# Six graph layers on one Trainium2 core: f32 queries and keys in the first attention, centring on GpSimd, and a new order of all parts

## What is computed

```python
h = jnp.maximum(_layernorm(x, axis=-1), 0.0)
x = x + _L0_gnn_ref(h, adj, ...)   # attention, 12 heads of 32, masked by adj, beta * adj added
h = jnp.maximum(_layernorm(x, axis=-1), 0.0)
x = x + _L1_gnn_ref(h, adj, ...)   # 2 layers: exp(h W h^T) * adj, one W above and one below the diagonal
h = jnp.maximum(_layernorm(x, axis=-1), 0.0)
x = x + _L2_gnn_ref(h, adj, ...)   # 2 layers: softmax(h h^T) * adj, three value matrices (upper, diagonal, lower)
h = jnp.maximum(_layernorm(x, axis=-1), 0.0)
x = x + _L3_gnn_ref(h, adj, ...)   # attention, 12 heads, adj as bias, output projection
```

```python
q = _split_heads(input_graph @ Wq + bq)
k = _split_heads(input_graph @ Wk + bk)
scores = jnp.einsum('bhqd,bhkd->bhqk', q, k) / jnp.sqrt(jnp.asarray(HD, input_graph.dtype))
scores = jnp.where(adj_e > 0, scores + beta * adj_e, -9e15)
probs = jax.nn.softmax(scores, axis=-1)
```

## Time and profile before

| | |
|---|---|
| median of 3 runs | 2869.08 us |
| the profiled execution | 2870.44 us, of which span of the instructions 2868.4 us |
| granted TensorE clock, mean over the span | 0.991 |
| PE busy | 2745.3 us, 96% |
| DVE busy | 2475.5 us, 86% |
| ACT busy | 1797.9 us, 63% |
| POOL busy | 1396.4 us, 49% |
| DMA | 125.40 MB, 44 GB/s |

### The profile page before, as it was taken

The page is one execution under the profiler, slowest core; times in us unless marked ns, Lnnn a source line. Parts: engine busy times, 40 slices in busy tenths (PEclk is TensorE's granted clock), DMA queues, the critical chain, the costliest instruction groups (busy, mean ns, idle before and its releaser), DMA issues.

```text
span 2868.4 us, 86681 instructions
## 1 busy us (share of the span) xinstructions
PE 2745.3 (96%) x33152; PEld 2100.0 (73%) x33152; DVE 2475.5 (86%) x6886; ACT 1797.9 (63%) x6516; POOL 1396.4 (49%) x2313
## 2 busy tenths in 40 slices
PE   3799999999999999999999999999999999999996
PEld 2577777777777777777777777777777777777763
DVE  6788888888888888888888888888888888888875
ACT  6566666666666666666666666666666666666653
POOL 0345554554544554554554554554455454554553
PEclk8999999999999999999999999999999999999998
DMA  6221121221212121121221222121121221121110
GB/s 199 57 38 40 39 42 40 38 42 41 37 43 42 36 45 39 36 45 39 36 45 39 36 45 40 39 42 40 39 42 40 39 42 39 36 45 40 36 32 20
DMA packets 343428, 125.40 MB, mean 44 GB/s; under 512 B 310896, under 2 KB 342896, under 8 KB 342896
## 3 DMA queue, kind: packets, MB, share of 16 engines
q1 hardware_dynamic: 333808, 107.28, 18.9%
q10 hardware_dynamic: 9216, 12.59, 1.2%
HBM read 31.72 MB, written 12.58 MB: 15 GB/s over the span
## 4 chain that ended last, share of the span: by engine, by line
PE 85%; DVE 6%; ACT 3%; issue 2%; POOL 2%; DMA 2%; SPq 0%; POOLq 0%; ACTq 0%; DVEq 0%
PE bank L925 63%; PE bank L1030 8%; PE bank L975 5%; PE bank L991 3%; PE bank L967 3%; DMA ht<-qk 1%; PE bank L1021 1%; ACT t L672 1%; DVE t L804 1%; PE bank L980 1%; PE bank L997 1%; DVE qk L782 1%; DMA row<-in_rows_dram 1%; DVE qk L750 1%; ACT qk L648 0%
## 5 line engine op out<-in xcount | busy, mean ns | idle before, releaser
L925 PE MATMUL bank<-w_hi,ht 128*128 128x384 f16 x3840 | 1028.6, 326 | 0.2 <-ACT v L639 0.2
L925 PE MATMUL bank<-ht,w_hi 128*128 128x128 f16 x9216 | 838.4, 220 | 17.1 <-DMA ht<-qk 15.3
L925 PE MATMUL bank<-ht,w_lo 128*128 128x128 f16 x4608 | 806.5, 220 | 0.0
L925 PEld LDWEIGHTS bank<-ht,w_hi 128*128 128x128 f16 x9216 | 725.9, 98 | 79.1 <-issue 33.8
L925 PE MATMUL bank<-w_lo,ht 128*128 128x384 f16 x1920 | 626.5, 326 | 0.0
L672 ACT ACTIVATE t<-t,few 128x128 f32<-128x128 f32 x1536 | 592.4, 389 | 6.8 <-DVE few L813 4.9
L925 PEld LDWEIGHTS bank<-w_hi,ht 128*128 128x128 f16 x3840 | 375.8, 98 | 232.8 <-issue 2.0
L925 PEld LDWEIGHTS bank<-ht,w_lo 128*128 128x128 f16 x4608 | 453.5, 98 | 0.0
L551 POOL TENSOR_TENSOR h<-h,row 128x384 f32<-128x384 f32 x256 | 258.0, 1008 | 242.8 <-DVE h L904 242.8
L663 ACT ACTIVATE qk<-bank 128x256 f16<-128x256 f32 x576 | 215.6, 381 | 234.9 <-PE bank L925 234.3
L541 POOL TENSOR_TENSOR v<-v,row 128x384 f32<-128x384 f32 x256 | 259.4, 1014 | 180.9 <-ACT v L639 180.9
(11 more groups left out here) (112 smaller groups left out, 5059.7 us busy)
## 6 DMA issues: line engine op xcount, KB each, us to landing
x<-in_x_dram SPq DMA_DIRECT2D x64, 192.0 KB, 2.3
out_dram<-h ACTq DMA_DIRECT2D x64, 192.0 KB, 2.2
ht<-qk SPq DMA_TRANSPOSE x384, 2.8
w_hi<-in_weights_dram SPq DMA_DIRECT2D x9, 576.0 KB, 5.1
w_lo<-in_weights_dram SPq DMA_DIRECT2D x8, 576.0 KB, 4.9
adj<-in_adj_dram SPq DMA_DIRECT2D x64, 64.0 KB, 2.2
row<-in_rows_dram SPq DMA_DIRECT2D x1, 3456.0 KB, 15.4
spare<-in_weights_dram SPq DMA_DIRECT2D x2, 576.0 KB, 5.0
```

Source lines behind the costliest of these rows:

```text
L925: m = nc.tensor.matmul(out, a, b, start=(first and n == 0), stop=(last and n == 3 * len(left) - 1))
```

## The change

1. **Queries and keys of the first attention stay f32.** ScalarE writes them with the bias as f32 into the same tile (`QF`, the f32 view of `QK`); VectorE has no part in these `proj` steps; the bank is released by ScalarE's signal; `scores` waits for that and makes one f32 matmul for each head, 12 in place of 36. Order strings of VectorE have three entries fewer for each graph.
2. **Centring by GpSimd.** The 24 + 8 additions of the negative mean go from ScalarE to a new `set_up` of GpSimd: first w5, then the eight rows, then w8 to w14.
3. **Two row DMAs.** The eight rows that are centred come in one DMA behind w2, with a semaphore of their own, the other ten in one behind w5.
4. **New order strings** for all engines, opening, body (11 times) and closing. In the opening, SyncE issues x and `adj` of streams 2, 1 and 0 right after the biases and ahead of all weights, and the first graph's turn ahead of w4; GpSimd's set-up pieces stand ahead of the first graph's value bias; the turns of graphs 1 and 2 and their loads on the other engines come earlier. In the body, TensorE's order now has `scale` and `mix` of the last attention side by side, `aturn`, the third `vals` and `context` of DIG_B one after the other, and `flip` ahead of `scores` of the last attention; GpSimd does the masks of DIG_B's `aturn` before the norm's addition of DIR_B.

```diff
+WHOLE_QK = (GAT,)
...
 OPENING = {
...
     "sync":
-        "wwwww0ww1wwww0wwwww4w120www032w101032102143",
+        "w210wwwww0wwwwwwww1w4w3w02www0w1w0103210241",
 }
...
-REPEATS = 10
+REPEATS = 11
...
     if name == "proj":
-        return ["high", "low"]
+        return ["high"] if layer in WHOLE_QK else ["high", "low"]
...
+        if name == "proj":
+            return layer not in WHOLE_QK
...
+    if name == "proj" and layer in WHOLE_QK:
+        return "high", step, 0
     return RELEASE[name], step, j if name == "scores" else 0
...
+        QF = [q.bitcast(F32).rearrange("p (c a t) -> p c a t", c=C, a=2) for q in flat_qk]
...
                     if w == 2:
-                        sp.dma_start(row[:, 1:N_ROWS], rows_v[:, 1:N_ROWS].broadcast_to((P, N_ROWS - 1, D))).then_inc(rows_in, 16)
+                        sp.dma_start(row[:, CENTRED_ROWS], rows_v[:, CENTRED_ROWS].broadcast_to((P, 8, D))).then_inc(value_rows_in, 16)
+                        yield
+                    if w == 5:
+                        sp.dma_start(row[:, 9:N_ROWS], rows_v[:, 9:N_ROWS].broadcast_to((P, N_ROWS - 9, D))).then_inc(rows_in, 16)
                         yield
...
+            def set_up():
+                for k, w in enumerate(CENTRED_W):
+                    pool.wait_ge(w_sums, 2 * k + 2)
+                    for c in range(C):
+                        mean = means[:, 8 + k * C + c:9 + k * C + c]
+                        nc.gpsimd.tensor_scalar(stage_of(w)[:, c], stage_of(w)[:, c], mean, None, ALU.add).then_inc(w_centred, 1)
+                    yield
+                    if k == 0:
+                        pool.wait_ge(row_sums, 2)
+                        for n in range(8):
+                            nc.gpsimd.tensor_scalar(row[:, 1 + n], row[:, 1 + n], means[:, n:n + 1], None,
+                                                    ALU.add).then_inc(rows_centred, 1)
+                        yield
...
                     if w in CENTRED_W:
-                        act.wait_ge(w_sums, 2 * CENTRED_W.index(w) + 2)
-                        for c in range(C):
-                            mean = means[:, 8 + CENTRED_W.index(w) * C + c:9 + CENTRED_W.index(w) * C + c]
-                            nc.scalar.activation(stage_of(w)[:, c], stage_of(w)[:, c], ACT.Identity,
-                                                 bias=mean).then_inc(w_centred, 1)
                         act.wait_ge(w_centred, C * (CENTRED_W.index(w) + 1))
...
+                        dst = QF[s] if layer in WHOLE_QK else QK[s][:, 0]
                         for side in range(2):
-                            last = nc.scalar.activation(QK[s][:, 0, i, side], bank_of(r, s, step)[:, side * TOK:(side + 1) * TOK],
+                            last = nc.scalar.activation(dst[:, i, side], bank_of(r, s, step)[:, side * TOK:(side + 1) * TOK],
                                                         ACT.Identity, bias=bias_qk[:, side, i:i + 1])
...
-                    wait_for(pe, r, s, "low", ("proj", layer, C - 1))
+                    wait_for(pe, r, s, "high" if layer in WHOLE_QK else "low", ("proj", layer, C - 1))
...
+                        if layer in WHOLE_QK:
+                            for h in range(HPC):
+                                rows_h = slice(HD * h, HD * (h + 1))
+                                m = nc.tensor.matmul(bank_of(r, s, step, h)[:, c * P:(c + 1) * P], QF[s][rows_h, c, 0, cols],
+                                                     QF[s][rows_h, c, 1, cols], start=True, stop=True)
+                                if c == C - 1:
+                                    m.then_inc(filled[s], 1)
+                            continue
```

More of the change, by code:

```diff
@@ L138 @@
+        "140002013104001324133104112341030030300341302323434201113124210112430244210223402141141411402413"
+        "434040312224230321223041300321334013202202022013024040101423330",
     "pool":
-        "001343321322142034433112404432433203140044223010043044314201100334121104100420312211440232210211"
-        "031423322",
+        "134302302211343232321240413413322404343432301024024433010404043412130130044121010104023241241100"
+        "232121210",
     "sync":
-        "20132043124310423042103410321402143",
+        "30213204132431024304213041032410214",
@@ new lines @@
+        "232231311202244411433340322311231131002122004444431343400033222322040444213422122434133331000200"
+        "144040144233134331010001034434030224423342211131100021210404243042411112333140044104143002203242"
+        "211323211130100300232220211120020011310333322233222111113333322332212121111333333222223333332222"
+        "2333332333333",
+    "vector":
+        "431133101343222240312112300211211444333123322421431332320032004442241423123334213422132322300204"
+        "442434020333434341430004321301304324414024330343423042003311401044134104003042422041411443100100"
+        "231304414043203440214112120142000413210102133103420021201011121200010030012322321230311102122123"
+        "2133011321312222321311211312333321221322332332122232333133232232223332333333332233333333323",
@@ L171 @@
[L171 to L172 removed]
+        "143323002211433231322042114343322044344332030104224433010040442431101330044121101002021231140023"
+        "21221131233220113323322231332323333323",
     "sync":
[L174 removed]
+        "320130243124130423042103413021021321323233",
 }
@@ L602, in step_of @@
                                             ALU.add).then_inc(done[s]["biased"], 1)
-            run("pool", step_of)
+            run("pool", step_of, set_up())
         @block.scalar
@@ L622, in set_up @@
                     yield
-                    if w == 2:
-                        act.wait_ge(row_sums, 2)
-                        for k in range(8):
-                            nc.scalar.activation(row[:, 1 + k], row[:, 1 + k], ACT.Identity,
-                                                 bias=means[:, k:k + 1]).then_inc(rows_centred, 1)
-                        yield
             def step_of(r, s, name, layer, i):
@@ L658, in step_of @@
                             act.wait_ge(bias_scaled, 1)
+                        dst = QF[s] if layer in WHOLE_QK else QK[s][:, 0]
                         for side in range(2):
-                            last = nc.scalar.activation(QK[s][:, 0, i, side], bank_of(r, s, step)[:, side * TOK:(side + 1) * TOK],
+                            last = nc.scalar.activation(dst[:, i, side], bank_of(r, s, step)[:, side * TOK:(side + 1) * TOK],
                                                         ACT.Identity, bias=bias_qk[:, side, i:i + 1])
                     else:
-                        last = nc.scalar.activation(QK[s][:, 0, i].rearrange("p a t -> p (a t)"), bank_of(r, s, step)[:, 0:2 * TOK], ACT.Copy)
+                        dst = QF[s] if layer in WHOLE_QK else QK[s][:, 0]
+                        last = nc.scalar.activation(dst[:, i].rearrange("p a t -> p (a t)"), bank_of(r, s, step)[:, 0:2 * TOK], ACT.Copy)
                     last.then_inc(done[s]["high"], 1)
```

65 lines of the change are left out of this document (21 added, 44 removed).

## The result

The changed kernel takes 2949.34 us (median of 4 runs, 2948.43 to 2951.09) beside 2869.49 us of before: ratio 1.0279, 95% interval 1.0263 to 1.0295. It is 80 us slower, 89 us above the forecast of 2860.7 and outside the range of 2838 to 2894. The profiled execution took 2951.09 us with 2949.3 us of span, at a granted clock of 0.988.

A forecast was written before the change was run, and what follows sets the result against it. PE, busy for 96% of the span, was taken as the bound. 2868.4 + 16.6 - 18 + 9 - 15 - 1 = 2860.0 us of span, giving a forecast of 2860.7 us, range 2838 to 2894.

The forecast's parts named there:

- f32 score step: First attention's scores on PE: 0.88 us a step, 0.26 more than before, over 64 graphs +16.6 us.
- (e): Rival: f32 weight loads of a row group don't hide behind its matmuls, +56 us, 2900 us; chance 0.09.
- (f): Rival: f32 weight loads of the four row groups follow one another, +125 us, 2970 us; chance 0.04.
- VectorE's relief: VectorE loses 384 low halves, 115.2 us in all; worth nearly nothing in the body.
- The stall of scale and context: Body: PE's wait for GpSimd's mask between scale and context, 0.34 us a graph, goes: -18 us.
- New seams: Body: new waits in PE's order, 0.15 us a graph over 57 graphs, +9 us, bounds 0 and +20.
- a microsecond of PE work less to hide behind: Body: thinner cover for the path from DIR_A's context to DIR_B's projection, within the 0.15 us a graph for seams.
- Opening: Opening: first projection at 18.6 to 20 us, first attention's end 14 us earlier; -15 us, bounds 0 and -25.
- Tail: Closing: last graph's projections and scores ahead of the last-but-one's final product, -1 us, bounds -5 and +5.
- (d): Rival: new seams as costly as the old one and an opening that gives nothing, +18.6, 2888 us; chance 0.10.

The follow-up runs named there:

- e2: Kernel before with only the f32 queries and keys of the first attention (12 f32 matmuls, no low halves on VectorE): 2879.05 us, ratio 1.0026.
- e4: Changed kernel with SyncE's turn ahead of the load in the body, and f16 halves with VectorE's low halves back in the first attention: 2937.39 us, ratio 1.0227.
- e1: Changed kernel with SyncE's DIG_A turn ahead of the load in the body, as in before: 2899.82 us, ratio 1.0098.
- e7: Kernel before with GpSimd's masks of DIG_B's attention put ahead of DIR_B's norm addition: ratio 1.0207.
- e16: Before with last attention's mix ahead of DIG_B's context, its value bias, DIG_A's norm and turn, and DIR_A's third low half moved earlier: ratio 1.0071.
- e10: e6 with GpSimd's value bias of the first attention moved from right behind DIR_A's to behind a later norm addition: 2873.83 us, ratio 1.0007.
- e3: Kernel before with the load ahead of the DIG_A turn in SyncE's body order, as in the changed kernel: 3154.05 us, ratio 1.0983.
- e6: e1 with DIR_B's turn moved earlier on ScalarE and VectorE: 2885.45 us, ratio 1.0057.
- e8: Kernel before with the changed kernel's opening, its order followed for the first 136 TensorE steps: 2867.23 us, ratio 0.9992.
- e5: Kernel before with the changed kernel's opening, its order followed for the first 184 TensorE steps: 2868.37 us, ratio 0.9996.

## Why the prediction was wrong, step by step

- **f32 score step, +16.6: right.** Timeline of PE in the changed kernel, as in the earlier trace rows:

```profile
1028.65 0.95 PE L971 MATMUL bank<-qk 32*128 32x128 f32 x24
1029.53 0.34 PE L929 MATMUL bank<-w_hi,ht 128*128 128x384 f16 x1
```

  0.88 us, the number forecast, and not by luck: the 0.08 us more than a mix sit where they were put, at the first load. From the first round of four matmuls to the second it takes 0.21 us, in a mix 0.13, and from each later round to the next 0.11 us in both (starts of the single records). Rivals (e) and (f) are out: six rounds whose loads have records of 186 ns fit in 0.88 us. The rule of the Trainium skill that was weighed there ("TensorE: Matmul & The Clock Gate", "The mechanism") would have made it 1.5 us; for these row-tiled f32 matmuls it doesn't hold. Nevertheless the part alone cost 7.5 us (e2), for the reason in the next point.
- **VectorE's relief, "worth nearly nothing": mis-sized.** It gave back some 9 us in before's order: 16.6 less 7.5. In the new strings it is worth more: without it, and with the cheaper f16 scores, e4 is 38 us slower than e1.
- **The stall of scale and context, -18: the gap closed, the gain wasn't there.** After has 0.20 us where before had 0.48. But e7 to e16 show that in before's order every kernel without the gap has it elsewhere, by the waits because VectorE has no room; and in the new order e10 has the same sum of seams as before. That PE waits for POOL was read rightly; what failed is that I didn't ask why GpSimd's mask took 0.60 us, or who else that order served.
- **New seams, +9 with bounds 0 and +20: the step that failed.** The body grew by 1.78 us a graph (1.74 over the table's graphs), all terms together, where 0.13 was put; of the 1.74, 0.27 are the score step. The largest part isn't a seam of PE at all. The text went through the queue of SyncE in the opening, and for the body through TensorE's and GpSimd's order only; SyncE's body string was never decoded. There a load that waits for the previous graph's x stood in front of a DMA that PE was about to need: 52 us (e1), and the same swap in before's order costs 282 us (e3). The second part was named ("a microsecond of PE work less to hide behind" for DIR_B's projection) and priced far too low: 0.4 us a graph above the 0.20 of a mix's seam, 13 us of it taken back by e6. The third, GpSimd's two additions back to back beside VectorE's low half, 13 us (e10), was not seen. Together 78 of the 80 us.
- **Opening, -15: right in kind, too large by more than half.** The first projection starts at 20.32 us (18.6 to 20 forecast). The first graph's attention ends with VectorE's addition to x at 55.3 us (54.77 + 0.56), where 48 to 49 were put and before had 62.9: 7.6 us, not 14. The term that was mis-sized is the centring, 1.2 to 1.7 us a piece with 0.5 to 1.0 taken. The mark that I had named is treacherous: the second graph's transpose of stream 0 is 16 us earlier (194.2 for 210.1 us), but the new strings simply have it at another place among the streams. PE's work done is the better mark: 7.8 us ahead at 200 us, and in e10, whose body loses least, 5.4 us at 500 us. So the opening is worth some 5 to 6 us in the changed strings (an estimate from this count), and 2.5 or less behind before's body (e8, e5).
- **Tail, -1**: right in sign. No run changed the closing alone; in e10 it wins back some 4 us by the count of steps.
- **Range and rivals.** All slower rivals were built from TensorE's side. A DMA held up in SyncE's queue by the wait of the DMA ahead of it had none, though the text ahead of the prediction says that every engine is strictly in order within its string. Among the rivals' sums, (d) is 1 us too high: the same terms give +17.6 and 2887 us.

No kernel here beats before clearly. The nearest is e8 (0.9992, interval to 1.0001).

## What to carry to other kernels

Decode the order string of every in-order queue that a change touches, the DMA-issuing one first: for each entry ask what it waits for and who needs the entry behind it. A wait on the bound engine may be what lets another engine run at full speed; before counting it as a gain, look whose instructions run beside it and at what speed, and whether a second engine has any slack in that stretch. Measure a lead by work done on the bound engine, not by the time of a milestone whose place in the order has changed.

## What the runs showed of the hardware

- f32 matmuls of 32 rows on four row groups: 12 of them (24 records) in 0.88 us from start to the next product, with load records of 186 ns (L971) that don't show.
- VectorE's operation with two SBUF inputs: 1.34 us (e7) and 1.36 us (e1) beside GpSimd's additions, 0.55 us (e10) behind them and 0.62 us (before) beside GpSimd's mask; that mask 0.60 us beside VectorE's addition (before), 0.29 us without it (e7). So either engine can be the one that is slowed.
- The same centring of 128x384 f32: 0.52 us from one to the next on ScalarE (before), 1.2 to 1.7 us on GpSimd (after).
- In e1 a transposing DMA without a code transfer beside it lands within 2.9 us (170 of 170); of 132 with one, 62 land after more than 3.5 us.
- In e3, where PE waits most, the mean granted clock was 0.960, against 0.991 in before.
- One DMA issue whose wait is not met holds up the issues behind it in SyncE's string: 472 us of such waiting at the load of x in after, and 52 us of the kernel's time.
